# A graph-attention layer with pre-norm: its beginning rearranged (small loads, normalization, first slab, first matmuls)

## The reference

```python
h = max(layernorm(x), 0)                       # over the last axis, no weights
q, k, v = h @ wq.T + bq, h @ wk.T + bk, h @ wv.T + bv
q2, k2, v2 = q @ wiq.T + biq, k @ wik.T + bik, v @ wiv.T + biv     # then split in heads
mask = full((384, 384), -inf); mask[src, dst] = softplus(edge_type_weights)[type - 1]
# a diagonal element without an edge gets softplus(edge_type_weights)[3]
attn = softmax(q2 @ k2.T / 8 + mask)           # for each head
y = x + (attn @ v2) @ wo.T + bo
```

## Time and profile before

| | |
|---|---|
| median of 3 runs | 304.92 us (304.61 to 304.93) |
| the profiled execution | 304.59 us |
| its span, first to last instruction | 302.8 us |
| TensorE matmul, weight load | 295.2, 270.4 us busy |
| VectorE, ScalarE, GpSimd | 179.8, 153.4, 149.3 us busy |
| granted TensorE clock | 1.00, full speed |
| moved by DMA | 40.82 MB, 135 GB/s in the mean |

### The profile page before, as it was taken

One profiled execution on the slowest core, in us unless ns is written; L12 is line 12 of the kernel. 1 busy time (PEld: TensorE's weight loads), 2 busy tenths in 40 slices (PEclk: granted clock), 3 DMA queues, 4 the chain that ended last, 5 costly groups with the idle time before them and its releaser, 6 DMA issues.

```text
span 302.8 us, 4742 instructions
## 1 busy us (share of the span) xinstructions
PE 295.2 (98%) x1707; PEld 270.4 (89%) x1707; DVE 179.8 (59%) x475; ACT 153.4 (51%) x288; POOL 149.3 (49%) x152
## 2 busy tenths in 40 slices
PE   6899999999999999999999999999999999999996
PEld 3689998888899999999999999999999998787886
DVE  3889978784544444344487756566665656647241
ACT  1886433252533344433345684949494949874100
POOL 5431544643465454555101993938383848964000
PEclk9999999999999999999999999999999999999999
DMA  6978875739533334443733133030313121400031
GB/s 187 391 207 257 276 229 197 215 127 349 207 139 107 111 133 139 139 132 103 252 105 124 28 125 128 8 135 16 124 28 114 55 85 65 146 0 2 0 139 69
DMA packets 15817, 40.82 MB, mean 135 GB/s; under 512 B 3481, under 2 KB 4914, under 8 KB 15794
## 3 DMA queue, kind: packets, MB, share of 16 engines
q1 hardware_dynamic: 13490, 39.29, 38.8%
q0 software_dynamic: 2016, 1.21, 1.6%
q10 hardware_dynamic: 288, 0.03, 0.1%
HBM read 37.71 MB, written 2.81 MB: 134 GB/s over the span
## 4 chain that ended last, share of the span: by engine, by line
PE 91%; DVE 3%; ACT 2%; DMA 1%; POOL 1%; issue 1%; SPq 0%
PE bank L805 26%; PE bank L809 25%; PE bank L806 25%; PE bank L923 5%; PE bank L908 4%; PE bank L938 3%; PE bank L939 3%; DMA x_sb<-in_x 1%; DVE a_lo L661 1%; DVE stats L633 1%; POOL rstd L347 1%; DVE prob L724 0%; PE bank L857 0%; ACT pt_hi L510 0%; ACT work L517 0%
## 5 line engine op out<-in xcount | busy, mean ns | idle before, releaser
L388 POOL DMA_INDIRECT cells<-value,cell x51 | 55.6, 1090 | 57.4 <-DMA cells<-value,cell 46.0
L805 PE MATMUL bank<-a_hi,w_hi 128*128 128x384 f32 x192 | 64.7, 337 | 0.0
L809 PE MATMUL bank<-a_lo,w_hi 128*128 128x384 f32 x192 | 64.4, 335 | 0.0
L806 PE MATMUL bank<-a_hi,w_lo 128*128 128x384 f32 x192 | 64.2, 334 | 0.0
L427 ACT ACTIVATE w_hi<-raw 128x1024 fp32r<-128x1024 f32 x51 | 54.0, 1058 | 19.1 <-PE bank L809 17.3
L668 DVE TENSOR_TENSOR w_lo<-raw,w_hi 128x1024 fp32r<-128x1024 f32 x36 | 44.0, 1223 | 15.2 <-ACT w_hi L427 14.6
L406 POOL TENSOR_SCALAR prob<-prob,row_inv 128x384 f32<-128x384 f32 x36 | 23.0, 646 | 41.5 <-DVE row_inv L734 41.5
L361 POOL TENSOR_TENSOR w_lo<-raw,w_hi 128x1024 fp32r<-128x1024 f32 x15 | 36.0, 2397 | 8.7 <-ACT w_hi L427 8.7
L805 PEld LDWEIGHTS bank<-a_hi,w_hi 128*128 128x128 f32 x192 | 36.0, 188 | 1.0 <-POOL w_lo L361 0.3
L809 PEld LDWEIGHTS bank<-a_lo,w_hi 128*128 128x128 f32 x192 | 36.0, 188 | 0.4 <-DVE a_lo L681 0.4
L806 PEld LDWEIGHTS bank<-a_hi,w_lo 128*128 128x128 f32 x192 | 36.1, 188 | 0.0
(11 more groups left out here) (135 smaller groups left out, 608.4 us busy)
## 6 DMA issues: line engine op xcount, KB each, us to landing
raw<-in_slabs SPq DMA_DIRECT2D x56, 512.0 KB
x_sb<-in_x SPq DMA_DIRECT2D x6, 256.0 KB, 4.8
work<-key_rows SPq DMA_DIRECT2D x6, 256.0 KB, 4.6
prob<-key_rows SPq DMA_DIRECT2D x6, 256.0 KB, 3.8
x_sb<-in_x SPq DMA_DIRECT2D x3, 512.0 KB, 5.8
out_y<-x_sb SPq DMA_DIRECT2D x5, 256.0 KB, 2.1
cells<-prob SPq DMA_DIRECT2D x2, 576.0 KB, 8.9
cells<-value,cell POOLq DMA_INDIRECT x51
```

Source lines behind the costliest of these rows:

```text
L388: nc.gpsimd.indirect_dma_start(out=cells[c][:, :], out_offset=bass.IndirectOffsetOnAxis(ap=cell[:, t:t + 1], axis=0), in_=value[:, t:t + 1 ...
L805: nc.tensor.matmul(psum, w[0], a[0], start=first, stop=False)
L806: nc.tensor.matmul(psum, w[1], a[0], start=False, stop=False)
L809: return nc.tensor.matmul(psum, w[0], a[1], start=False, stop=last)
```

## The change

Nine edits, all in the first part of the programs:

- SP loads the edge weights, biases, rows and columns behind slab 1 (before: the first two on ScalarE's queue at the start, the others behind slab 0).
- SP waits for the row of keys behind slab 3 (before: slab 2) and reads unit n of keys behind slab n + 4 (before: n + 3).
- GpSimd makes the keys after slab 1's low part (before: right after the last power).
- GpSimd makes both low parts of slab 0; half 0 waits for the last shift as well.
- VectorE makes slab 0's second high half, by a copy, after its part of h (before: ScalarE, between high parts of h).
- VectorE's part of the last row tile: max(x - mean, 0) first, in one instruction that needs no rstd, then the multiplication with rstd.
- ScalarE's part of it in two pieces of 256 columns, and TensorE turns two blocks after each.
- TensorE: no warm-up matmuls after the last row tile; blocks 4 to 6 of it are turned between the second and third matmul of tile 0; tile 0 has its own function.
- The units of edges are taken in the order 6, 0, 7, 1, ... (before 0, 6, 1, 7, ...), and the first scatter waits for the scaled weights (`sp_ok`), not for the edges' values; the later ones wait for the values.

Since slab 0's second high half no longer counts in `slab_hi`, the waits on it drop by one. The diff, with most unchanged lines left out:

```diff
--- before.py
+++ after.py
@@ -50,13 +50,13 @@
...
-WARM = [18, 4, 3, 2]
+WARM = [18, 4, 3]
 TILES_AHEAD = 3
...
 LATE = CHAIN - NT
-UNIT_ORDER = [0, 6, 1, 7, 2, 8, 3, 9, 4, 10, 5, 11, 12]
+UNIT_ORDER = [6, 0, 7, 1, 8, 2, 9, 3, 10, 4, 11, 5, 12]
 assert 2 * CHAIN == NT + ET and LATE == 6 * EG and sorted(UNIT_ORDER) == list(range(GROUPS))
@@ -189,7 +189,7 @@
...
         h_turned, h_hi, h_lo = sem("h_turned"), sem("h_hi"), sem("h_lo")
-        half_hi, half_lo = sem("half_hi"), sem("half_lo")
+        half_hi, half_lo, early_hi = sem("half_hi"), sem("half_lo"), sem("early_hi")
         slab_hi, slab_lo, slab_lo_dve, slab_used = sem("slab_hi"), sem("slab_lo"), sem("slab_lo_dve"), sem("slab_used")
@@ -291,7 +291,10 @@
...
                 sp_eng.dma_start(raw[:, s % RAW, :], slabs[s]).then_inc(slab_in[s % RAW], 16)
-                if s == 0:
+                if s == 1:
+                    sp_eng.dma_start(ew[:], edge_weights.rearrange("(a n) -> a n", a=1).to_broadcast([P, 4])).then_inc(
+                        ew_in, 16)
+                    sp_eng.dma_start(bias[:], biases).then_inc(small_in, 16)
                     for i in range(2):
@@ -299,14 +302,15 @@
...
                         sp_eng.dma_start(cell_rows(c), prob[:, c]).then_inc(filled, 16)
+                if s == 3:
                     sp_eng.wait_ge(key_row_ok, 1)
                     sp_eng.dma_start(key_rows[0, :].rearrange("(t e) -> t e", e=P), key_row[:]).then_inc(keys_out, 16)
-                if 3 <= s < 3 + GROUPS:
-                    if s == 3:
+                if 4 <= s < 4 + GROUPS:
+                    if s == 4:
                         sp_eng.wait_ge(keys_out, 16)
-                    elif s == 9:
+                    elif s == 10:
                         sp_eng.wait_ge(filled, 32)
-                    load_keys(s - 3)
+                    load_keys(s - 4)
                 if s == Q0 + 2:
@@ -347,16 +351,9 @@
...
-            pool.wait_ge(rows_in, 32)
-            nc.gpsimd.tensor_copy(rows[:], rows_i[:]).then_inc(rows_ok, 1)
-            pool.wait_ge(rows_ok, 1)
-            nc.gpsimd.tensor_scalar(key_row[:], rows[:, 0, :], float(N), 0.0, ALU.mult, ALU.add).then_inc(rows_ok, 1)
-            pool.wait_ge(rows_ok, 2)
-            nc.gpsimd.tensor_tensor(key_row[:], key_row[:], rows[:, 1, :], ALU.add).then_inc(key_row_ok, 1)
             def split_lo(s):
-                pool.wait_ge(slab_hi, s + 1)
+                pool.wait_ge(slab_hi, s)
                 hi, lo = split_place(s)
@@ -365,16 +362,18 @@
...
-            half = slice(HALF, F)
-            pool.wait_ge(slab_hi, 1)
-            nc.gpsimd.tensor_tensor(w_lo[:, 0, half], raw[:, 0, half], w_hi[:, 0, half].bitcast(F32),
-                                    ALU.subtract).then_inc(slab_lo, 1)
+            pool.wait_ge(shift_ok, NT)
+            for b in range(2):
+                half = slice(b * HALF, (b + 1) * HALF)
+                pool.wait_ge((half_hi, early_hi)[b], 1)
+                nc.gpsimd.tensor_tensor(w_lo[:, 0, half], raw[:, 0, half], w_hi[:, 0, half].bitcast(F32),
+                                        ALU.subtract).then_inc((half_lo, slab_lo)[b], 1)
...
                     pool.wait_ge(filled, 32)
-                    pool.wait_ge(value_ok, 1)
+                    pool.wait_ge(sp_ok, 1)
                     pool.wait_ge(dump_ok, 1 + NT)
@@ -384,12 +383,21 @@
...
                 t = i - NT if c == 0 else LATE + i
+                pool.wait_ge(value_ok, 1)
                 pool.wait_ge(cell_ok, UNIT_ORDER.index(t // EG) + 1)
...
             split_lo(1)
+            pool.wait_ge(rows_in, 32)
+            nc.gpsimd.tensor_copy(rows[:], rows_i[:]).then_inc(rows_ok, 1)
+            pool.wait_ge(rows_ok, 1)
+            nc.gpsimd.tensor_scalar(key_row[:], rows[:, 0, :], float(N), 0.0, ALU.mult, ALU.add).then_inc(rows_ok, 1)
+            pool.wait_ge(rows_ok, 2)
+            nc.gpsimd.tensor_tensor(key_row[:], key_row[:], rows[:, 1, :], ALU.add).then_inc(key_row_ok, 1)
             done = 0
@@ -431,29 +439,24 @@
...
-            def first_slab_hi(b):
-                half = slice(b * HALF, (b + 1) * HALF)
+            def first_slab_hi():
+                half = slice(0, HALF)
                 act.wait_ge(slab_in[0], 16)
-                nc.scalar.activation(w_hi[:, 0, half], raw[:, 0, half], ACT.Copy).then_inc((half_hi, slab_hi)[b], 1)
-            act.dma_start(ew[:], edge_weights.rearrange("(a n) -> a n", a=1).to_broadcast([P, 4])).then_inc(ew_in, 16)
-            act.dma_start(bias[:], biases).then_inc(small_in, 16)
+                nc.scalar.activation(w_hi[:, 0, half], raw[:, 0, half], ACT.Copy).then_inc(half_hi, 1)
             for t in range(NT):
                 if t == NT - 1:
-                    first_slab_hi(0)
+                    first_slab_hi()
                 act.wait_ge(shift_ok, t + 1)
-                part = slice(0, F) if t < NT - 1 else slice(0, HALF)
-                nc.scalar.activation(x_sb[:, t, part], x_sb[:, t, part], ACT.Relu, scale=rstd[:, t:t + 1],
-                                     bias=shift[:, t:t + 1]).then_inc(h_ok, 1)
+                for part in [slice(0, F)] if t < NT - 1 else [slice(b * HALF // 2, (b + 1) * HALF // 2) for b in range(2)]:
+                    nc.scalar.activation(x_sb[:, t, part], x_sb[:, t, part], ACT.Relu, scale=rstd[:, t:t + 1],
+                                         bias=shift[:, t:t + 1]).then_inc(h_ok, 1)
             for k in range(KT):
...
                 nc.scalar.activation(a_hi[:, k, :], h_bank[k][:, 0:N], ACT.Copy).then_inc(h_hi, 1)
-                if k == 1:
-                    first_slab_hi(1)
-                if k == 4:
+                if k == KT // 2:
                     split_hi(1)
@@ -637,18 +640,15 @@
...
                 nc.vector.tensor_scalar(var_eps[:, t:t + 1], mean_var[:, t, 1:2], EPS, None, ALU.add).then_inc(var_ok, 1)
+            h_last = x_sb[:, NT - 1, HALF:F]
+            nc.vector.tensor_scalar(h_last, h_last, mean_var[:, NT - 1, 0:1], 0.0, ALU.subtract,
+                                    ALU.max).then_inc(h_step, 1)
             shift_part(NT - 1)
-            h_last = x_sb[:, NT - 1, HALF:F]
-            dve.wait_ge(shift_ok, NT)
-            nc.vector.tensor_scalar(h_last, h_last, rstd[:, NT - 1:NT], shift[:, NT - 1:NT], ALU.mult,
-                                    ALU.add).then_inc(h_step, 1)
             dve.wait_ge(h_step, 1)
-            nc.vector.tensor_scalar(h_last, h_last, 0.0, None, ALU.max).then_inc(h_last_ok, 1)
-            half = slice(0, HALF)
-            dve.wait_ge(half_hi, 1)
-            nc.vector.tensor_tensor(w_lo[:, 0, half], raw[:, 0, half], w_hi[:, 0, half].bitcast(F32),
-                                    ALU.subtract).then_inc(half_lo, 1)
+            nc.vector.tensor_scalar(h_last, h_last, rstd[:, NT - 1:NT], None, ALU.mult).then_inc(h_last_ok, 1)
+            dve.wait_ge(slab_in[0], 16)
+            nc.vector.tensor_copy(w_hi[:, 0, HALF:F], raw[:, 0, HALF:F]).then_inc(early_hi, 1)
@@ -663,7 +663,7 @@
...
-                dve.wait_ge(slab_hi, s + 1)
+                dve.wait_ge(slab_hi, s)
                 hi, lo = split_place(s)
@@ -798,14 +798,10 @@
...
         def _(pe):
-            def products(psum, w, a, first, last, h_tiles=0):
-                if h_tiles:
-                    pe.wait_ge(h_hi, h_tiles)
+            def products(psum, w, a, first, last):
                 nc.tensor.matmul(psum, w[0], a[0], start=first, stop=False)
                 nc.tensor.matmul(psum, w[1], a[0], start=False, stop=False)
-                if h_tiles:
-                    pe.wait_ge(h_lo, h_tiles)
                 return nc.tensor.matmul(psum, w[0], a[1], start=False, stop=last)
@@ -814,12 +810,7 @@
...
-                if t == 0 and ks[-1] < KT // 2:
-                    pe.wait_ge(half_lo, 1)
-                    hi, lo = split_place(0)
-                else:
-                    hi, lo = split_slab(slab_of(t))
+                hi, lo = split_slab(slab_of(t))
                 if t > 3 * KT + 4:
@@ -828,7 +819,7 @@
...
                     mm = products(psum[:, 0:N], (hi[:, c], lo[:, c]), (a_h[:, k, :], a_l[:, k, :]), k == 0,
-                                  k == KT - 1, k + 1 if t == 0 else 0)
+                                  k == KT - 1)
                 if k == KT - 1:
@@ -862,19 +853,40 @@
...
             pe.wait_ge(ident_ok, 1)
-            for t in range(NT):
+            for t in range(NT - 1):
                 pe.wait_ge(h_ok, t + 1)
                 for k in range(KT - 1):
-                    if t == NT - 1 and k == HALF // P:
-                        pe.wait_ge(h_last_ok, 1)
                     turn_h(k, t)
                 warm(WARM[t + 1])
-            for k in range(KT):
-                tile(0, a_hi, a_lo, [k])
-                if k == 0:
-                    for t in range(NT):
-                        turn_h(KT - 1, t)
+            for b in range(2):
+                pe.wait_ge(h_ok, NT + b)
```

(24 more changed lines are left out.)

## The result

| | before | changed |
|---|---|---|
| median (7 runs each) | 304.92 us | 307.06 us |
| lowest to highest | 304.32 to 305.26 | 306.25 to 309.56 |
| ratio, 95% interval | | 1.0093 (1.0073 to 1.0112) |
| profiled execution, its span | 304.59, 302.8 us | 306.25, 304.4 us |
| mean granted TensorE clock over the 7 runs | | 0.999 once, 0.989 to 0.994 six times |

The change makes the kernel slower by 2 us, where 0.3 us less was forecast.

What follows compares the result with a forecast made beforehand. TensorE, 98% busy, bounds, with VectorE close behind at tiles 3 and 4. Tile 1 gains 0.68 + 0.45 = 1.1 us, 0.8 is given back at tile 3, 0.3 kept: 304.92 - 0.3 = 304.6 us; range 303.6 to 305.9.

Steps and rivals of the forecast that it cites:

- rival B: Ahead of the first edge unit: keys arrive late and VectorE waits; 305.9 us taken, 307.1 in the worse working; chance 0.14.
- the keys' round trip: Keys written to DRAM and read back before the first edge unit: 25.0 to 31.8 us, 25.1 taken.
- x's 0.45: Loads of x at the start: moving the small loads closes a DMA hole, 0.45 us gained of at most 0.78.
- when VectorE is ready: Ahead of the first edge unit: VectorE ready at 25.03 us, before the 0.45 us from x's earlier arrival.
- the 0.75 for collisions with GpSimd: After slab 1's low part: GpSimd's key instructions delay VectorE on the shared port, 0.35 to 1.0 us, 0.75 taken.
- the signs of being wrong: Listed signs against the forecast, among them the first eviction or slab 3 or 4 holding up an engine.
- the 0.15 us at tiles 3 and 4: VectorE's low parts end 0.15 us ahead of TensorE's starts there, so TensorE's gain needs VectorE's too.
- the gain at tile 1 behind the shift: Slab 1's low part ends at 18.06 instead of 18.74 us, so tile 1 gains 0.68 us.
- The forecast's 0.06 for power and shift: Last row tile: shift 0.17 us shorter, up to 0.1 returned by subtraction beside the power; shift ends 0.06 us earlier.
- Rival C: At VectorE's tensor_scalar of the edge values: scatter 0's indirect DMA holds the port, 1.2 us more, 305.7 us; chance 0.08.
- The mask: New unit order and earlier self-loop scatters only move the mask; VectorE's score steps show no wait: 0 us.

Runs made afterwards that it cites:

- the last version: Changed kernel with rows and keys made in two earlier GpSimd gaps, and VectorE's edge units behind the next tile's low part: 303.64 us, ratio 0.9973.

## Why the prediction was wrong

The mechanism that decided was on the list as rival B, with a chance of 0.14; its worse working gave 307.1, and I took its lesser one, 305.9, for the price and for the end of the range.

**The step that failed** is the keys' round trip: "25.0 at the least, 31.8 at the most", "so I take the lower durations: 25.1". With x's 0.45 that put the first unit at 24.65; it came at 26.57. By its own terms: key_row was ready at 19.41, where the least gave 18.97 (L397 had the collision with slab 2's low part that I had named and left out of the value), +0.44; from there to the issue of the read 1.70 passed, for 2.1 forecast for the write, -0.40; the read took 5.46 for 3.5, +1.96. The last is the size that was wrong. I took the least row of the keys' reads, and the five reads that VectorE waited for took 4.72 to 5.76. Why they take longer than 3.5 stays open. With the middles of my own two ranges the forecast would have been B.

**Near by luck: when VectorE is ready.** Forecast 24.58, measured 26.57 - 2.53 = 24.04, of which 0.30 is the shift (10.70 for the forecast 11.00). But the 0.75 for collisions with GpSimd was mis-sized. From GpSimd's release to readiness VectorE took 24.04 - 17.22 = 6.82 us, 0.60 more than the 6.22 of before, and 0.52 of that is the wait for slab 3 at 19.77; collisions are about 0.1. That slab 3 could hold up an engine was among the signs of being wrong and had no price.

**A wrong reading: the 0.15 us at tiles 3 and 4.** The prediction took the time from the end of VectorE's low part to TensorE's start for VectorE's lead. The same 0.15 passes in the changed kernel where TensorE had waited 2.96 us (28.67 to 28.82), so it is what the hand-over takes. TensorE's last matmuls ahead of tiles 3 and 4 in the kernel before:

```profile
27.05 0.34 PE L809 MATMUL bank<-a_lo,w_hi 128*128 128x384 f32 x1
...
31.30 0.34 PE L809 MATMUL bank<-a_lo,w_hi 128*128 128x384 f32 x1
```

The tiles start 0.18 and 0.19 us behind them (27.23, 31.49), its usual pace within 0.02: TensorE hardly waits, and VectorE is just in time, with no lead. The sum is the same by this, for it gave tile 3 only what VectorE gained.

**A term was missing**: TensorE's clock behind a wait. It took 1.5 us in the execution where it shows, and a mean clock of 0.994 or less is in eight of the changed kernel's eleven runs. How much of the rest of the way, from the profiled 306.25 to the median of 307.06, is the clock and how much a later arrival of x stays open: a run with a clock of 0.994 took 306.53 us, and the matmuls in the wait left runs at 307.3 and 307.6 with the full clock.

**Right**: the gain at tile 1 behind the shift, 0.62 of the forecast 0.68 (the other 0.06 was the shift's own) against 0.68 measured (1.49, less the 0.81 by which the shift ended earlier); tile 0 ending together with slab 1's low part; VectorE as the engine at tiles 3 and 4 through which every gain has to pass, in keeping with the last version, where TensorE's waits are gone with the units out of the way; the port: L575 took 0.70 us beside GpSimd again, and L397 1.21. Both follow the rule of the Trainium skill, "SBUF — State Buffer" (section "SBUF: two separate sides"), that whoever starts first holds the pair: once GpSimd did (14.80 to 17.22), once VectorE (17.50 to 18.71). The forecast's 0.06 for power and shift did not come: the shift took 0.17 less, and the power beside the subtraction 0.17 more.

**Not borne out**: x's 0.45 us. It was read from one hole in one trace. In the changed kernel's first profile the last statistics start 0.81 us earlier (8.59 for 9.40), but over fourteen profiles they start at 9.19 with the small loads moved and at 9.28 without, and the two experiments on the small loads show no gain in the median.

**Rival C** is out: the indirect DMA (L381) ran from 23.04 to 24.30, and the tensor_scalar (L626) that started beside it at 23.54 took 0.25 us. In this row it did not hold VectorE up as L361 held L572, and the 305.7 by the page's rule did not come about.

**The mask** was priced at nothing because VectorE's score steps (L724) showed no wait for it. The step that reads the table is another, L673, and it idled 0.26 us for it in the same trace; the experiment with the small loads shows 4.59 us of wait in another execution. With some 7 us from the read's issue to its use (146.04 to 153.3) and single reads that differ by microseconds, its slack belonged in the working and the range.

## What to carry to other kernels

When a step is moved back, follow it to its last user and price the whole trip, the DRAM write, SP's order and the read back included, with the typical row under the load that will be there and not with the least one; here a forecast wait of less than 0.1 us became 2.53. An engine that hands its part over just in time is a second bottleneck: work that can wait goes behind the step that the bottleneck needs, which gave the lowest median here. The time from one engine's end to the other's start is no lead; compare it with the same distance at a place where the other did wait. A gain that rests on when a DMA lands has to be looked at in several executions.
